# Gated cross-attention: transposes by VectorE and a DRAM round trip in place of TensorE's, and attend in the middle of a step

## The chip, the cores and the metric

One core of a Trainium2 chip. Time is device microseconds of one execution, the median of the runs.

## What is computed

For each of 32 batches, 112 rows of x (512 wide) attend to 375 rows of memory (256 wide), and a gate mixes the result into x. The reference, cut to what matters:

```
memory_proj    = einsum('bme,de->bmd', memory, W_mem)
scores         = einsum('bnd,bmd->bnm', hidden_states, memory_proj) / sqrt(D)
attn           = softmax(scores, axis=-1)
memory_context = einsum('bnm,bmd->bnd', attn, memory_proj)
gate_input     = concatenate([hidden_states, memory_context], axis=-1)
gate           = sigmoid(einsum('bnf,df->bnd', gate_input, W_gate) + b_gate)
fused          = hidden_states + gate * memory_context
out            = rmsnorm(fused, norm_w)        # eps 1e-6
```

All arrays are float32.

## The kernel before

memory_proj is never formed. W_mem is folded into the other side: q = x W_mem, scores = q memory^T, am = softmax(scores) memory (256 wide), context = am W_mem^T, and the gate's attended half is am times wga, a product of the two weights that is made once at the start.

**Precision.** Each float32 operand of a product is split into a high part (ScalarE, `high`) and the remainder (VectorE or GpSimd, `low`, a tensor_tensor that subtracts). Each product is three: high by high, high by low, low by high. A name with `_hi` or `_lo` is such a part, `_raw` what it is made from, and the name without either the thing itself. GpSimd makes memT_lo, mem_lo (one pair a batch) and xT_lo (three units a group); VectorE makes qT_lo, pT_lo and amT_lo.

**Tiling.** Eight batches of 112 rows make a group of 896 columns, which is seven tiles of 128 rows. Scores, softmax and attend go by batch; the gate, context, fuse and norm go by tile. Tile t of a group needs batches up to t+1. There are four groups; the two in the middle are one loop body. q is made in six pieces a group (three units of 256, 320 and 320 columns, two halves each).

**One step of TensorE (batch b)**, in the order in which `group` and `fillers` write it: `score(b)`, `gate_x(b-1)` (the x half of a gate, twelve products), `probs_turn(b)` (three transposes of the probabilities through an identity), `gate_am(b-2)` (the attended half, six products), `attend(b)` (nine products), `context(b-2)` (six), `am_turn(b)` (two transposes). q pieces stand where there is no tile work.

**The other engines in that step.** VectorE: gate_context (work from ctx_ps), amT_low, maximum (top and shift), fuse (work from x_rows), shares (a reciprocal), pT_low, add_bias (work from gate_ps), norm (work from rstd and norm_w), and q_low where there is a piece. ScalarE: the high parts, the exponential with its sum, the scaled copy `am`, tanh and the square with its sum. GpSimd: memT_lo, the inverse root, mem_lo, xT_lo. SP issues all DMAs in one list: a batch's memory (760 KB, both layouts in one transfer), x rows, results, xT.

Each engine runs its own list in order; what ties them are semaphores with constant thresholds (or registers in the loop body). `pT_low` and `amT_low` read the transposes where TensorE left them, in PSUM (`pT_ps`, `am_bank`).

## Time and profile before

| | us |
|---|---|
| median of 3 runs | 296.33 (296.28 to 297.29) |
| span of the profiled execution | 294.5 |
| TensorE busy | 287.4 |
| VectorE busy | 190.2 |
| ScalarE busy | 171.9 |
| GpSimd busy | 161.5 |

The profile is one execution. Its span runs from the first to the last instruction; the timed runs lie 1.8 us above it, which is what surrounds the span. An engine's busy time is the sum of its instructions; neighbouring matrix products overlap, so a group's mean is longer than the pace at which they follow each other. That pace is read from the chain of waits in order of time. The granted clock is the share of TensorE's full speed that the chip allowed in a stretch.

### The profile page before, as it was taken

How to read it: one execution, taken by the hardware profiler on the slowest of the kernel's cores; microseconds unless marked ns; L12 is line 12 of the kernel's file. 1: busy time of each engine (PE TensorE's matmuls, PEld its weight loads, DVE VectorE, ACT ScalarE, POOL GpSimd, SP SyncE). 2: the span in 40 equal slices, each digit the busy share in tenths (PEclk: the TensorE clock that was granted, in tenths of full speed). 3: DMA queues.
4: the chain of work that ended last, by engine and by line, in shares of the span. 5: the costliest groups of instructions: out<-in, count | busy, mean ns of one | idle time of the engine just before them, and what ended most of it. 6: DMA issues, size and time to landing. Idle time of an engine off the chain costs nothing.

```text
span 294.5 us, 4927 instructions
## 1 busy us (share of the span) xinstructions
PE 287.4 (98%) x1639; PEld 251.4 (85%) x1639; DVE 190.2 (65%) x328; ACT 171.9 (58%) x363; POOL 161.5 (55%) x132
## 2 busy tenths in 40 slices
PE   8999999999999999999999999999999999999991
PEld 4989888888899988888899988888889998888881
DVE  3897556787663267687674247777667335787755
ACT  4886757667447555657636555757735656555442
POOL 0002774859828535858945545685981943555312
PEclk9999999999999999999999999999999999999998
DMA  7997357557452634637472550757654233543101
GB/s 277 421 353 233 116 202 267 177 180 241 137 172 71 250 107 123 236 119 255 160 248 71 175 188 25 266 177 235 208 172 147 102 111 106 179 153 97 38 36 71
DMA packets 15571, 50.83 MB, mean 173 GB/s; under 512 B 1729, under 2 KB 1985, under 8 KB 15297
## 3 DMA queue, kind: packets, MB, share of 16 engines
q1 hardware_dynamic: 15552, 50.60, 51.1%
q8 instruction: 10, 0.16, 0.2%
q14 instruction: 9, 0.07, 0.1%
HBM read 43.25 MB, written 7.34 MB: 172 GB/s over the span
## 4 chain that ended last, share of the span: by engine, by line
PE 98%; issue 0%; DVE 0%; DVEq 0%; POOL 0%; POOLq 0%; ACT 0%
PE gate_ps L283 14%; PE gate_ps L285 14%; PE gate_ps L290 13%; PE ctx_ps L290 5%; PE ctx_ps L283 5%; PE ctx_ps L285 5%; PE q_ps L290 4%; PE q_ps L285 4%; PE q_ps L283 4%; PE am_bank L290 4%; PE am_bank L285 4%; PE am_bank L283 4%; PE score_ps L283 4%; PE score_ps L290 4%; PE score_ps L285 4%; PE pT_ps L335 3%
## 5 line engine op out<-in xcount | busy, mean ns | idle before, releaser
L855 POOL TENSOR_TENSOR memT_lo<-mems_raw,memT_hi 128x752 fp32r<-128x752 f32 x30 | 56.2, 1873 | 75.6 <-ACT memT_hi L513 75.6
L855 POOL TENSOR_TENSOR mem_lo<-mems_raw,mem_hi 128x768 fp32r<-128x768 f32 x30 | 56.2, 1873 | 3.5 <-ACT mem_hi L513 3.5
L638 ACT ACTIVATE am<-am_bank,share 112x256 f32<-112x256 f32 x32 | 15.2, 475 | 44.7 <-PE am_bank L290 44.7
L716 DVE SCALAR_TENSOR_TENSOR work<-work,x_rows 128x512 f32<-128x512 f32 (+1 forms) x29 | 40.6, 1404 | 0.6
L670 DVE TENSOR_TENSOR pT_lo<-pT_ps,pT_hi 128x336 fp32r<-128x336 f32 x32 | 16.2, 508 | 35.8 <-ACT pT_hi L513 35.8
L724 DVE SCALAR_TENSOR_TENSOR work<-work,rstd,norm_w 128x512 f32<-128x512 f32 (+1 forms) x29 | 35.2, 1217 | 1.0 <-POOL rstd L916 1.0
L283 PE MATMUL gate_ps<-wgx_hi,xT_hi 128*128 128x512 f32 x112 | 32.5, 399 | 0.0
L285 PE MATMUL gate_ps<-wgx_lo,xT_hi 128*128 128x512 f32 x112 | 31.7, 391 | 0.0
L290 PE MATMUL gate_ps<-wgx_hi,xT_lo 128*128 128x512 f32 x112 | 31.6, 391 | 0.0
L538 ACT ACTIVATE probs<-score_ps,shift 112x375 f32<-112x375 f32 x32 | 18.4, 574 | 22.4 <-DVE shift L684 22.3
L873 POOL TENSOR_TENSOR guarded<-meansq,eps 128x1 f32<-128x1 f32 x27 | 5.1, 189 | 45.9 <-ACT work L545 45.9
L545 ACT ACTIVATE work<-work 128x512 f32<-128x512 f32 (+1 forms) x29 | 17.8, 614 | 21.2 <-DVE work L716 21.2
L855 POOL TENSOR_TENSOR xT_lo<-xT_raw,xT_hi 128x1280 fp32r<-128x1280 f32 (+1 forms) x9 | 29.1, 3230 | 0.0
L709 DVE SCALAR_TENSOR_TENSOR work<-work,ctx_ps 128x512 f32<-128x512 f32 (+1 forms) x28 | 19.0, 677 | 13.9 <-PE ctx_ps L290 12.8
L513 ACT ACTIVATE memT_hi<-mems_raw 128x752 fp32r<-128x752 f32 x32 | 26.4, 826 | 1.0 <-DMA mems_raw<-in_mems 1.0
L513 ACT ACTIVATE mem_hi<-mems_raw 128x768 fp32r<-128x768 f32 x32 | 26.8, 837 | 0.0
L285 PEld LDWEIGHTS gate_ps<-wgx_lo,xT_hi 128*128 128x128 f32 x112 | 21.0, 188 | 4.7
L290 PEld LDWEIGHTS gate_ps<-wgx_hi,xT_lo 128*128 128x128 f32 x112 | 21.0, 188 | 4.6
L703 DVE TENSOR_TENSOR work<-gate_ps,b_gate 128x512 f32<-128x512 f32 (+1 forms) x29 | 19.4, 670 | 7.2 <-PE gate_ps L290 7.1
L670 DVE TENSOR_TENSOR amT_lo<-am_bank,amT_hi 128x224 fp32r<-128x224 f32 x32 | 12.4, 387 | 17.9 <-ACT amT_hi L513 17.9
L682 DVE TENSOR_REDUCE top<-score_ps 112x1 f32<-112x375 f32 x32 | 17.5, 548 | 8.5 <-PE score_ps L290 8.4
L283 PEld LDWEIGHTS gate_ps<-wgx_hi,xT_hi 128*128 128x128 f32 x112 | 19.8, 188 | 1.8
(123 smaller groups left out, 653.1 us busy)
## 6 DMA issues: line engine op xcount, KB each, us to landing
mems_raw<-in_mems SPq DMA_DIRECT2D x32, 760.0 KB, 4.5
x_rows<-in_x SPq DMA_DIRECT2D x28, 256.0 KB, 4.9
out<-work SPq DMA_DIRECT2D x27, 256.0 KB, 5.0
xT_raw<-in_xT SPq DMA_DIRECT2D x7, 640.0 KB, 5.7
xT_raw<-in_xT SPq DMA_DIRECT2D x3, 512.0 KB, 5.1
work<-in_wgT SPq DMA_DIRECT2D x1, 1024.0 KB, 7.2
x_rows<-in_wgT SPq DMA_DIRECT2D x1, 1024.0 KB, 10.3
xT_raw<-in_xT SPq DMA_DIRECT2D x2, 320.0 KB, 5.0
```

What stands on the lines that cost most here:

```text
L283: pe.matmul(out, l_hi, r_hi, start=first and i == 0, stop=False)
L285: pe.matmul(out, l_hi, r_lo, start=False, stop=False)
L290: mm = pe.matmul(out, l_lo, r_hi, start=False, stop=last and i == len(lefts) - 1)
L513: return act.activation(out, in_, ACT.Copy)
L538: act.activation(probs[:, b % 2, 0:KEYS], scores[:, 0:KEYS], ACT.Exp, bias=shift[:, b % 2:b % 2 + 1], scale=D ** -0.5, accum_out=total[:, ...
L545: act.activation(squares[:, cols], h[:, t % 2, cols], ACT.Square, scale=D ** -0.5, accum_out=meansq[:, slot:slot + 1]).then_inc(meansq_rea ...
L670: return dve.tensor_tensor(out, in_, high.bitcast(F32), ALU.subtract)
L703: dve.tensor_tensor(z[:, t % 2, cols], gate_ps[t % 2][:, cols], b_gate[:, cols], ALU.add).then_inc(z_ready, 1)
L709: dve.scalar_tensor_tensor(out=u[:, cols], in0=z[:, t % 2, cols], scalar=1.0, in1=bank[:, cols], op0=ALU.add, op1=ALU.mult).then_inc(u_rea ...
L716: dve.scalar_tensor_tensor(out=h[:, t % 2, cols], in0=u[:, cols], scalar=0.5, in1=x_rows[:, t % X_SLOTS, cols], op0=ALU.mult, op1=ALU.add) ...
L724: dve.scalar_tensor_tensor(out=y[:, t % 2, cols], in0=h[:, t % 2, cols], scalar=rstd[:, t % 2:t % 2 + 1], in1=norm_w[:, cols], op0=ALU.mul ...
L855: return pool.tensor_tensor(out, in_, high.bitcast(F32), ALU.subtract)
```

## The change

Both transposes leave TensorE. VectorE transposes within blocks of 32 x 32 (`turn_p`, `turn_am`) and writes them in an order that makes the rest a matter of whole rows; SP writes that to a scratch tensor in DRAM and reads it back with the blocks at their places (`write_p`, `read_p`, `write_am`, `read_am`). The result lands in partitions in the order (row in block, block), so the host lays memory and W_mem out in the same order (`turned_rows`). ScalarE and VectorE then split `pT_raw` and `amT_raw` from SBUF, 384 columns in place of 336 and 256 in place of 224.

```diff
-            def probs_turn(g, b):
-                pe.wait_ge(probs_ready, GROUP * g + b + 1)
-                for c in range(KC):
-                    mm = pe.transpose(probsT[:, c], probs[:, b % 2, c * P:(c + 1) * P], ident[0:ROWS, 0:ROWS])
-                mm.then_inc(pT_done, 1)
...
-            def am_turn(g, b):
-                pe.wait_ge(am_ready, GROUP * g + b + 1)
-                for c in range(EC):
-                    mm = pe.transpose(amT_ps[:, c], am[:, c * P:(c + 1) * P], ident[0:ROWS, 0:ROWS])
-                mm.then_inc(amT_done, 1)
...
+            def turn_p(n):
+                dve.wait_ge(probs_ready, n + 1)
+                if n > 0:
+                    dve.wait_ge(p_written, 16 * n)
+                dve.transpose(turned_p, probs_blocks).then_inc(blocks_p_ready, 1)
...
+            def turn_am(n):
+                dve.wait_ge(am_ready, n + 1)
+                if n > 0:
+                    dve.wait_ge(am_written, 16 * n)
+                dve.transpose(turned_am, am_blocks).then_inc(blocks_am_ready, 1)
...
+            def write_p(n):
+                sp.wait_ge(blocks_p_ready, n + 1)
+                sp.dma_start(turned_p_d[n % 2], blocks_p[:]).then_inc(p_written, 16)
+
+            def read_p(n):
+                sp.wait_ge(p_written, 16 * (n + 1))
+                if n >= 1:
+                    sp.wait_ge(pT_lo_ready, n)
+                sp.dma_start(pT_flat, turned_p_d[n % 2].rearrange("(q i) (j n) -> (i j) q n", q=Q, j=Q)).then_inc(p_read, 16)
...
-            dve.wait_ge(pT_hi_ready, GROUP * g + b + 1)
-            low(pT_lo[:, b % 2], probsT, pT_hi[:, b % 2]).then_inc(pT_lo_ready, 1)
+                dve.wait_ge(pT_hi_ready, n + 1)
+                low(pT_slot(pT_lo, n), pT_rows, pT_slot(pT_hi, n)).then_inc(pT_lo_ready, 1)
```

The groups are no longer loops. Steps are numbered through from 0 to 34, batch s has its scores in step s, and its attend in step s + 1. The tile finished in step s is t = `tile_at(s)`: none where s mod 8 is 3. PSUM has a third gate bank in place of `pT_ps`, so that gate_x can run two tiles ahead. TensorE's steps, then VectorE's and SP's:

```diff
+            for s in range(OPENING, STEPS):
+                t = tile_at(s)
+                if s < BATCHES:
+                    score(s)
+                if t is not None and t + 2 < ALL_TILES:
+                    gate_x(t + 2)
+                if s <= BATCHES:
+                    attend(s - 1)
+                for g, unit, half in q_pieces_at(s):
+                    q_piece(g, unit, half)
+                if t is not None:
+                    gate_am(t)
+                    if t < LAST:
+                        context(t)
...
+            for s in range(OPENING, STEPS):
+                if tile_at(s - 2) is not None:
+                    finish(tile_at(s - 2))
+                if s - 2 < BATCHES:
+                    write_am(s - 2)
+                    read_am(s - 2)
+                if s < BATCHES:
+                    write_p(s)
+                if s + 2 < BATCHES:
+                    load_memT(s + 2)
+                if s + 1 < BATCHES:
+                    load_mem(s + 1)
+                if s < BATCHES:
+                    read_p(s)
+                if x_load_at(s) is not None and s != 2:
+                    load_xT(*x_load_at(s))
```

q pieces stand at s mod 8 = 0, 1, 3 (two), 6 and 7. GpSimd splits a unit of xT at s mod 8 = 1, 4 and 7. In the opening the memory loads come earlier, `load_memT(2)` ahead of wgx and of xT's third unit, and the first scores stand between the products of the weights. At the end, attend(31) stands in step 32 and gate_am of the last tile in step 34.

TensorE, one step in the middle of a group with a tile and no q piece, before (L283, L285 and L290 are the high-high, high-low and low-high products of every kind):

```order
L283 MATMUL score_ps<-memT_hi,qT_hi 112x376 x2
L285 MATMUL score_ps<-memT_lo,qT_hi 112x376 x2
L290 MATMUL score_ps<-memT_hi,qT_lo 112x376 x2
L283 MATMUL gate_ps<-wgx_hi,xT_hi 128x512 x4
L285 MATMUL gate_ps<-wgx_lo,xT_hi 128x512 x4
L290 MATMUL gate_ps<-wgx_hi,xT_lo 128x512 x4
L335 MATMUL pT_ps<-ident,probs 128x112 x3
L283 MATMUL gate_ps<-wga_hi,amT_hi 128x512 x2
L285 MATMUL gate_ps<-wga_lo,amT_hi 128x512 x2
L290 MATMUL gate_ps<-wga_hi,amT_lo 128x512 x2
L283 MATMUL am_bank<-mem_hi,pT_hi 112x256 x3
L285 MATMUL am_bank<-mem_lo,pT_hi 112x256 x3
```

and now, from score on:

```order
L353 MATMUL score_ps<-memT_hi,qT_hi 112x376 x2
L355 MATMUL score_ps<-memT_lo,qT_hi 112x376 x2
L360 MATMUL score_ps<-memT_hi,qT_lo 112x376 x2
L353 MATMUL gate_ps<-wgx_hi,xT_hi 128x512 x4
L355 MATMUL gate_ps<-wgx_lo,xT_hi 128x512 x4
L360 MATMUL gate_ps<-wgx_hi,xT_lo 128x512 x4
L353 MATMUL am_bank<-mem_hi,pT_hi 112x256 x3
L355 MATMUL am_bank<-mem_lo,pT_hi 112x256 x3
L360 MATMUL am_bank<-mem_hi,pT_lo 112x256 x3
L353 MATMUL q_ps<-xT_hi,wm_hi 128x256 x4
L355 MATMUL q_ps<-xT_lo,wm_hi 128x256 x4
L360 MATMUL q_ps<-xT_hi,wm_lo 128x256 x4
```

The transposes are gone, and attend stands ahead of the gate's attended half (here with a q piece between them).

VectorE, from gate_context of one tile to the pT_lo behind it, before:

```order
L709 SCALAR_TENSOR_TENSOR work<-work,ctx_ps 128x512
L670 TENSOR_TENSOR amT_lo<-am_bank,amT_hi 128x2x112
L681 REGISTER_ALU
L682 TENSOR_REDUCE top<-score_ps 112x1
L684 TENSOR_SCALAR shift<-top 112x1
L716 SCALAR_TENSOR_TENSOR work<-work,x_rows 128x512
L689 RECIPROCAL share<-total 112x1
L670 TENSOR_TENSOR pT_lo<-pT_ps,pT_hi 128x336
```

and now:

```order
L737 SCALAR_TENSOR_TENSOR work<-work,ctx_ps 128x512
L722 STREAM_TRANSPOSE blocks_am<-am 128x2x4x32
L688 TENSOR_TENSOR amT_lo<-amT_raw,amT_hi 128x2x128
L700 TENSOR_REDUCE top<-score_ps 112x1
L702 TENSOR_SCALAR shift<-top 112x1
L744 SCALAR_TENSOR_TENSOR work<-work,x_rows 128x512
L708 STREAM_TRANSPOSE blocks_p<-probs 128x3x4x32
L712 RECIPROCAL share<-total 112x1
L688 TENSOR_TENSOR pT_lo<-pT_raw,pT_hi 128x384
```

Two block transposes stand in that stretch that were not there, and amT_lo and pT_lo read SBUF where they read PSUM; pT_lo is that of the batch before.

SP, one step with a load of xT in it, before:

```order
L200 DMA mems_raw<-in_mems 128x1520
L196 DMA xT_raw<-in_xT 128x1280
L210 DMA x_rows<-in_x 128x512
L250 DMA out<-work 128x512
L200 DMA mems_raw<-in_mems 128x1520
```

and a step now:

```order
L268 DMA x_rows<-in_x 128x512
L275 DMA out<-work 128x512
L259 DMA turned_am<-blocks_am 128x256
L265 DMA amT_raw<-turned_am 128x4x64
L249 DMA turned_p<-blocks_p 128x384
L240 DMA memT_raw<-in_memT 128x752
L245 DMA mem_raw<-in_mem 128x768
L255 DMA pT_raw<-turned_p 128x4x96
```

Each read-back waits on SP for its write to land, and the next write stands behind it.

## Rows read from the trace of the kernel before

**Rows 1.** The page: TensorE's busy time, share and instructions; its granted clock by slice
```profile
PE 287.4 (98%) x1639; PEld 251.4 (85%) x1639; DVE 190.2 (65%) x328; ACT 171.9 (58%) x363; POOL 161.5 (55%) x132
PEclk9999999999999999999999999999999999999998
```
**Rows 2.** The page: the chain that ended last, share of the span by engine
```profile
PE 98%; issue 0%; DVE 0%; DVEq 0%; POOL 0%; POOLq 0%; ACT 0%
```
**Rows 3.** The same chain in order of time: start us, us on the path, engine and tile
```profile
61.67 0.35 PE score_ps L283 x2
...
62.72 0.92 PE gate_ps L283 x4
...
65.45 0.29 PE pT_ps L335 x3
...
67.14 0.35 PE am_bank L283 x3
...
68.20 0.45 PE ctx_ps L283 x2
...
69.56 0.19 PE am_bank L354 x2
...
77.86 0.49 PE q_ps L283 x4
...
83.49 0.59 PE q_ps L283 x4
...
147.10 0.49 PE q_ps L283 x4
```
**Rows 4.** The timeline of one step: start us, us, engine, line, operation, [idle before]
```profile
200.08 0.68 DVE L709 SCALAR_TENSOR_TENSOR work<-work,ctx_ps 128x512 f32<-128x512 f32 x1
...
201.24 0.55 DVE L682 TENSOR_REDUCE top<-score_ps 112x1 f32<-112x375 f32 x1 [0.18 <-PE score_ps L290]
...
201.35 1.81 POOL L855 TENSOR_TENSOR memT_lo<-mems_raw,memT_hi 128x752 fp32r<-128x752 f32 x1 [1.75 <-ACT memT_hi L513]
...
201.82 0.15 DVE L684 TENSOR_SCALAR shift<-top 112x1 f32<-112x1 f32 x1
...
202.00 1.71 DVE L716 SCALAR_TENSOR_TENSOR work<-work,x_rows 128x512 f32<-128x512 f32 x1
...
202.01 0.58 ACT L538 ACTIVATE probs<-score_ps,shift 112x375 f32<-112x375 f32 x1 [0.74 <-DVE shift L684]
...
205.66 0.69 DVE L703 TENSOR_TENSOR work<-gate_ps,b_gate 128x512 f32<-128x512 f32 x1 [0.32 <-PE gate_ps L290]
...
206.27 1.45 DVE L724 SCALAR_TENSOR_TENSOR work<-work,rstd,norm_w 128x512 f32<-128x512 f32 x1
```
**Rows 5.** VectorE's timeline between two groups, where GpSimd has nothing to subtract
```profile
152.03 0.74 DVE L724 SCALAR_TENSOR_TENSOR work<-work,rstd,norm_w 128x512 f32<-128x512 f32 x1
...
153.75 0.68 DVE L716 SCALAR_TENSOR_TENSOR work<-work,x_rows 128x512 f32<-128x512 f32 x1
```
**Rows 6.** VectorE's groups by form: xcount | busy us, mean ns | idle before
```profile
L670 DVE TENSOR_TENSOR pT_lo<-pT_ps,pT_hi 128x336 fp32r<-128x336 f32 x32 | 16.2, 508 | 35.8 <-ACT pT_hi L513 35.8
...
L670 DVE TENSOR_TENSOR mem_lo<-mems_raw,mem_hi 128x768 fp32r<-128x768 f32 x2 | 1.9, 948 | 0.0
...
L734 DVE CAST xT_hi<-first_raw 128x512 fp32r<-128x512 f32 x1 | 0.4, 428 | 3.3 <-DMA first_raw<-in_first 3.3
```
**Rows 7.** DMA queues (packets, MB, busy share) and issues (KB each, us to landing)
```profile
q1 hardware_dynamic: 15552, 50.60, 51.1%
...
out<-work SPq DMA_DIRECT2D x27, 256.0 KB, 5.0
...
out<-work SPq DMA_DIRECT2D x2, 128.0 KB, 1.7
```
**Rows 8.** The timeline: the first split of wgx, and the last gate's products
```profile
14.53 1.14 ACT L513 ACTIVATE wgx_hi<-x_rows 128x512 fp32r<-128x512 f32 x2
...
286.54 0.62 PE L290 MATMUL gate_ps<-wga_hi,amT_lo 128*128 128x512 f32 x2
```

845 lines of the change are left out of this document (425 added, 420 removed).

## The prediction

> **What bounds the kernel now.** I read the busy shares first. TensorE is busy for 98% of the span, VectorE for 65%, ScalarE for 58%, GpSimd for 55%, and TensorE's granted clock stands at its upper level throughout [rows 1]. Then the chain of waits that ends last: TensorE has 98% of it, waiting and issuing nothing [rows 2]. So the kernel is TensorE's instruction list laid end to end, and what leaves that list shortens it, provided that nothing else becomes late. One step (a batch with a tile, without a q piece) takes 8.1 us (score at 61.67, the next behind the transposes at 69.56 + 0.19) and a group of eight batches 69.24 us (77.86 to 147.10), in the chain's order of time [rows 3]. Last I read VectorE's timeline: how long its chain from one gate to the next probabilities is, and what stretches it [rows 4, 5].
>
> **What is removed.** Per batch three transposes of probs (0.29 us) and two of am (0.19 us) on the path: 0.48 us, by 32 batches 15.4 us [rows 3]. TensorE's own work is then 7.62 us in a plain step (score 3 x 0.35, gate_x 3 x 0.92, attend 3 x 0.35, gate_am and context 3 x 0.46 each, less rounding), 65.4 in a group (69.24 - 8 x 0.48). The Trainium skill ("VectorE: DVE Perf Modes", section The three transpose paths) gives a TensorE transpose of 128x128 as 390 ns and VectorE's 32x32-block form as 311 ns, and its rules say to transpose 128x128 on TensorE where PSUM will do. The trace has them at 0.29 / 3 = 0.10 us each on the path, so by the page's figure 62 us would be won, by the row a quarter of it. The row decides.
>
> **What is added on VectorE.** Per batch a block transpose of 384 columns and one of 256. No row shows one. From below the CAST of 512 columns at 428 ns bounds it (384 columns: about 0.33 us). From above two passes over the data: the 768-column subtraction from SBUF at 948 ns (256 columns: 0.68). I take one pass, as VectorE's tensor_tensor rows go, 508 ns for 336 columns and 690 for 512, so 1.04 ns a column: 0.56 and 0.42 us [rows 4, 6]. pT_lo grows from 336 columns to 384 (0.56) and amT_lo from 224 to 256 (0.42), and both now read two SBUF tensors, where they read PSUM and SBUF.
>
> That last point has a price that the rows show. fuse and norm read two SBUF tensors. With GpSimd idle they take 0.68 and 0.74 us [rows 5]. With a GpSimd subtraction under way, fuse started at 202.00 ended at 203.71, that is 0.55 us behind the end (201.35 + 1.81) of memT_lo, and norm took 1.45 [rows 4]. add_bias and gate_context, which read PSUM, stay at 0.69 beside the same GpSimd work. So a two-SBUF operation waits until GpSimd's instruction ends. The block transposes have one input and should not.
>
> **What the new order does.** Before, gate_am(b-2) and a half of the gate stand between the probabilities and attend. Now attend(s-1) stands behind score(s) and gate_x(t+2), and VectorE issues pT_low(s-1) behind maximum(s), fuse, turn_p(s) and shares(s). So a loop closes every step: attend, gate_am, context, then VectorE's gate_context down to pT_low, then attend again. I lay it out from zero = end of gate_am(t-1), with the durations above; instructions back to back start 0.08 before the end of the last (205.66 + 0.69 = 206.35, next at 206.27) [rows 4].
> - TensorE: context ends 1.38, score(s) 2.42, gate_x 5.19, the six attend products that need no pT_lo 5.89.
> - VectorE: add_bias 0.04 to 0.73; norm to 1.40; gate_context waits for context, 1.42 to 2.11; turn_am to 2.46; amT_low to 2.80; maximum and shift to 3.45.
> - ScalarE: tanh to 1.4, am 1.8, amT_hi 2.1, memT_hi 2.85; exp 3.46 to 4.14 with its accumulator read.
> - GpSimd starts memT_lo(s+1) at 2.85 and holds until 4.67. fuse, ready at 3.48, ends 4.67 + 0.55 = 5.22. turn_p 5.14 to 5.71, the reciprocal hidden but for 0.08, pT_low(s-1) 5.71 to 6.27.
> - TensorE's last three attend products thus start at 6.3 in place of 5.89, and with gate_am's 1.38 the next zero is at 8.2.
>
> So the plain step takes 8.2 us, where TensorE alone wants 7.62 and before took 8.10: the saving is gone. A q piece lies inside the loop and adds its own 1.77 (3 x 0.59) or 1.45 us (3 x 0.49) [rows 3] to both sums, 10.0 and 9.65.
>
> Two places in a group are worse. **The step without a tile** (s mod 8 = 3) has neither gate_x nor gate_am. VectorE's pT_low(2) still comes at 6.27, while TensorE is through at 3.1; then two q pieces, their q_low and norm on VectorE, and score, gate_x, attend and gate_am of the next step. From gate_am(2) to gate_am(4) I get 17.2 us against 13.3 of TensorE's own. **The splits of xT** on GpSimd (3.4 us each, behind mem_lo) at s mod 8 = 1 and 7 reach 2.2 to 2.4 us past the next zero. norm waits for them, gate_context stands behind norm, amT_low then meets memT_lo: 1.3 and 1.4 us more. The one at 4 has no norm behind it and costs nothing.
>
> A group: 8.2 (s = 5) + 9.5 (2) + 11.4 (0) + 10.0 (1) + 2 x 9.65 (6, 7) + 17.2 (3 and 4) = 75.6 us, against 69.24.
>
> **The round trips.** turn_p(s) ends at 5.71; ScalarE wants its copy behind exp(s+1), at 8.2 + 4.15, so 6.6 us are there. A store of 128 KB with the queue empty lands 1.7 us after issue, one of 256 KB behind other loads 5.0 [rows 7]. So write plus read take 3.4 to 10 us. I take 5.5: the write 2.2, the read 3.3, as 760 KB of memory are issued ahead of it and the 50.6 MB so far keep the queues 51% busy (at that pace 760 KB take 2.3 us). That is hidden with 1.1 us to spare. SP's list is in order too: behind write_am(s-2) and its landing stands write_p(s). read_am is issued at about 5.1, before write_p is due. The second trip (am) has a whole step and is hidden, except at the end.
>
> **Opening.** load_memT(2) waits for VectorE's split of memT(0) (about 11 us) and stands ahead of the loads of wgx and xT unit 2, so wgx, split from 14.53 on before [rows 8], arrives at about 16. TensorE's list up to gate_am(0) sums to 40.3 us; I add 5.7 for gate_x(0) (0.8), attend(0) and q piece 2 (1.9) and score(3), whose memory split stands behind read_p(1) on ScalarE (3). So 46.
>
> **Tail.** After attend(31) nothing covers the trip of am: am, block transpose, write, read, two copies take until 8.4 us past gate_am(25) and the last three gate products 0.6 more. Before, the last gate ended at 286.54 + 0.62 = 287.2 [rows 8], 7.3 before the end of the span, and that part is unchanged.
>
> **The sum.** 46 + 27.5 (s = 5, 6, 7) + 3 x 75.6 - 2.9 (no q pieces in the last group) + 6.6 (s = 32) + 9.0 + 7.3 = 320.3 us of span. The medians lie 1.8 above the profiled span (296.3 against 294.5): **322 us**.
>
> **Rivals.**
> 1. *TensorE stays the bound, as intended: faster.* If turn_p(s) or pT_low is never late, each group costs 65.4. With opening and tail as above that is 290, with a clean opening 284: take **288**. It decides when pT_low(s-1) ends before 5.9 in the step. For it: TensorE never waited before, and VectorE idled 35.8 us before pT_lo alone [rows 6]. Against it: that idle time was 1.1 us a step, and the change puts 0.56 + 0.42 us of transposes into just that stretch.
> 2. *The waits for GpSimd fall elsewhere: about even.* If fuse meets no GpSimd work, pT_low ends at 5.3 and plain steps run at 7.62, but the step without a tile still loses 2.2. The group is 67.8, the total **297**, hence no change. It decides when memT_lo(s+1) begins after fuse.
> 3. *The round trip becomes the bound.* At 10 us, two trips of the loop take 10 + 0.55 + 0.56 + 0.54 + 1.38 + 5.71 = 18.7, or 9.4 a step, 1.2 over mine, by 28 steps +33: **355**. For it: 21 MB more through the queues, half of it in pieces of 384 and 256 bytes, and five more issues a step on SP. Against it: the 1.7 us row.
> 4. *Block transposes at their other bounds.* 0.33 and 0.3 us make it 314, 0.95 and 0.68 make it 340.
>
> **Chances.** My forecast, rival 4 inside it (305 to 335): 0.47. Rival 3, 335 and above: 0.20. Rival 2 (293 to 305): 0.13. Rival 1 (282 to 293): 0.20. The range of 286 to 345 leaves out a third of rival 1 and half of rival 3. A measurement of this kernel can tell about 0.5%, 1.5 us. Faster by more: 0.20 plus a fifth of rival 2, 0.23. Within: 0.07. Slower: 0.70.
>
> **What would show it.** Right: TensorE busy under 92%; waits of am_bank products for VectorE's pT_lo of about 0.4 us in plain steps and 3 us once in eight; pT_lo and amT_lo with means over their 0.56 and 0.42; VectorE over 80% busy. Rival 1: TensorE at 98% again. Rival 3: ScalarE's pT_hi waiting for the DMA of pT_raw. A granted clock below its upper level in mid-kernel would add to any of them and is in none of my numbers.

## The result and the profile of the changed kernel

The changed kernel takes 358.5 us (median of 6 runs, 354.4 to 360.5) against 296.3 before: 1.205 times as long, 95% interval 1.200 to 1.211. The direction of the prediction (slower) was right; its time, 322 us, was not, and its range ended at 345. The profiled execution took 354.4 us with a span of 352.3, so the sum to compare with is the predicted span, 320.3: 32.0 us are unexplained. Ratios and intervals here and below are over the fast runs, those within 1.5% of a kernel's fastest, and for an experiment without its profiled run, so they need not equal the quotient of two medians, and one experiment has too few such runs for any.

The page of the changed kernel, busy times and granted clock in 40 slices, then the chain that ended last by engine and its largest DMA shares (before: [rows 1, 2]):

```profile
PE 294.3 (84%) x1479; PEld 248.5 (71%) x1479; DVE 213.3 (61%) x388; ACT 172.9 (49%) x363; POOL 163.7 (46%) x135
...
PE   8939759999799769889799769888979779989973
...
PEclk9996998999899899999999989999989988999998
...
DMA packets 63191, 71.87 MB, mean 204 GB/s; under 512 B 37056, under 2 KB 45504, under 8 KB 62912
...
PE 29%; DMA 23%; DVE 21%; issue 16%; ACT 7%; SPq 2%; DVEq 0%; POOL 0%; POOLq 0%; ACTq 0%
```

TensorE fell from 98% busy to 84% though it has 160 instructions fewer, and from 98% of the chain to 29%. No engine took its place: VectorE is busy 61%. The path now goes round through all of them, with DMA in it for 23%. TensorE's busy time even rose, from 287.4 to 294.3 us, without the 15 us of transposes: its clock was granted at the lower level for part of the time (mean 0.953 against 0.995).

The waits: engine, line, tile, what was waited for; us in total, times, longest. First the engines', then SyncE's own:

```profile
PE am_bank L353 <- ACT pT_hi L532: 33.5, 19, 4.7
...
ACT memT_hi L532 <- DMA memT_raw<-in_memT: 12.1, 9, 2.1
...
ACT amT_hi L532 <- DMA amT_raw<-turned_am: 8.1, 3, 5.3
...
ACT pT_hi L532 <- DMA pT_raw<-turned_p: 7.5, 7, 1.9
PE am_bank L360 <- DVE pT_lo L688: 7.0, 13, 0.9
...
PE gate_ps L353 <- DVE wgx_lo L688: 5.5, 1, 5.5
```

```profile
SPq L265 <- DMA turned_am<-blocks_am: 84.5, 31, 6.5
SPq L275 <- DVE work L752: 51.6, 21, 5.4
SPq L255 <- DMA turned_p<-blocks_p: 27.6, 31, 6.3
```

TensorE waits at attend's first product, and mostly for ScalarE's pT_hi, not for VectorE's pT_lo as I had it. SyncE spends 112 us of the span waiting for a write to land before it may issue the read of the same rows (L265, L255).

Where the 32.0 us are, by the starts of add_bias on VectorE's timeline (each is the end of a gate_am):

| stretch | predicted | measured |
|---|---|---|
| to gate_am(0), step 4 | 46 | 57.7 |
| steps 5, 6, 7 | 8.2 + 9.65 + 9.65 = 27.5 | 8.4 + 9.8 + 9.8 = 27.9 |
| steps 8 to 31 | 3 x 75.6 - 2.9 = 223.9 | 82.7 + 81.9 + 78.8 = 243.4 |
| step 32, last gates, tail | 6.6 + 9.0 + 7.3 = 22.9 | 7.3 + 8.7 + 7.3 = 23.3 |

So the misses are the opening (11.7 us) and 6.5 us in each group.

### The profile page after: what moved, and what is told of

Its sections match the earlier page's. It is cut to its first block, busy times and chain, and to the rows that moved or that the text cites. A ratio compares the mean times of both kernels' runs of the same rounds, so it can differ in the third digit from the quotient of the medians.

```text
span 352.3 us, 4693 instructions
## 1 busy us (share of the span) xinstructions
PE 294.3 (84%) x1479; PEld 248.5 (71%) x1479; DVE 213.3 (61%) x388; ACT 172.9 (49%) x363; POOL 163.7 (46%) x135
## 2 busy tenths in 40 slices
DMA packets 63191, 71.87 MB, mean 204 GB/s; under 512 B 37056, under 2 KB 45504, under 8 KB 62912
## 4 chain that ended last, share of the span: by engine, by line
PE 29%; DMA 23%; DVE 21%; issue 16%; ACT 7%; SPq 2%; DVEq 0%; POOL 0%; POOLq 0%; ACTq 0%
DMA turned_am<-blocks_am 9%; DMA turned_p<-blocks_p 7%; DMA pT_raw<-turned_p 5%; PE am_bank L360 4%; PE gate_ps L353 3%; DVE work L731 3%; PE q_ps L355 3%; PE q_ps L353 3%; PE gate_ps L360 3%; PE gate_ps L355 3%; PE q_ps L360 3%; ACT work L588 3%; DVE top L700 3%; DVE blocks_am L722 3%; DVE blocks_p L708 3%
## 5 line engine op out<-in xcount | busy, mean ns | idle before, releaser
L872 POOL TENSOR_TENSOR memT_lo<-memT_raw,memT_hi 128x752 fp32r<-128x752 f32 x31 | 58.1, 1873 | 100.7 <-ACT memT_hi L532 100.7
L872 POOL TENSOR_TENSOR mem_lo<-mem_raw,mem_hi 128x768 fp32r<-128x768 f32 x32 | 59.7, 1864 | 16.6 <-ACT mem_hi L532 16.6
L353 PE MATMUL am_bank<-mem_hi,pT_hi 128*112 128x256 f32 x96 | 18.9, 307 | 33.5 <-ACT pT_hi L532 33.5
L353 PEld LDWEIGHTS am_bank<-mem_hi,pT_hi 128*112 128x112 f32 x96 | 14.1, 182 | 42.4 <-ACT pT_hi L532 41.2
L688 DVE TENSOR_TENSOR qT_lo<-q_ps,qT_hi 128x320 fp32r<-128x320 f32 (+1 forms) x22 | 10.4, 472 | 51.6 <-ACT qT_hi L532 51.5
L532 ACT ACTIVATE memT_hi<-memT_raw 128x752 fp32r<-128x752 f32 x32 | 26.4, 826 | 12.1 <-DMA memT_raw<-in_memT 12.1
L532 ACT ACTIVATE qT_hi<-q_ps 128x320 fp32r<-128x320 f32 (+1 forms) x22 | 9.3, 421 | 37.3 <-PE q_ps L360 36.7
L532 ACT ACTIVATE mem_hi<-mem_raw 128x768 fp32r<-128x768 f32 x32 | 26.6, 830 | 0.0
L360 PE MATMUL am_bank<-mem_hi,pT_lo 128*112 128x256 f32 x96 | 19.9, 320 | 7.1 <-DVE pT_lo L688 7.0
L708 DVE STREAM_TRANSPOSE blocks_p<-probs 128x384 f32<-128x384 f32 x32 | 18.3, 572 | 12.0 <-ACT probs L561 7.6
```

What stands on the lines that cost most here:

```text
L353: pe.matmul(out, l_hi, r_hi, start=first and i == 0, stop=False)
L360: mm = pe.matmul(out, l_lo, r_hi, start=False, stop=last and i == len(lefts) - 1)
L532: return act.activation(out, in_, ACT.Copy)
L708: dve.transpose(turned_p, probs_blocks).then_inc(blocks_p_ready, 1)
L872: return pool.tensor_tensor(out, in_, high.bitcast(F32), ALU.subtract)
```

## The experiments

The whole table first; "group" is the mean of the three times from the first gate of a group to the first of the next, and "first gate" the start of the first add_bias, both from VectorE's timeline of the one profiled run. With the trips in, the three differ (72.5, 79.2 and 79.3 us in the run G, 75.4, 81.6 and 73.3 in G, O); without them they agree to 0.2 us, but for T, O (73.0, 74.6 and 74.5). O: pT's split first on ScalarE and VectorE. G: GpSimd's work cut short. T: no round trips.

| run | us (range of runs) | ratio to before, interval | first gate | group |
|---|---|---|---|---|
| before | 296.3 | | 34.9 | 69.2 |
| changed | 358.5 (354.4 to 360.5) | 1.205, 1.200 to 1.211 | 57.7 | 82.2 |
| O | 342.3 (337.1 to 346.2) | 1.159, 1.152 to 1.166 | 54.6 | 77.9 |
| G | 339.9 (336.3 to 343.6) | none | 56.6 | 77.0 |
| T | 341.7 (339.7 to 342.8) | 1.152, 1.147 to 1.157 | 47.5 | 82.0 |
| G, O | 339.8 (339.2 to 340.8) | 1.145, 1.142 to 1.147 | 58.5 | 76.8 |
| T, O | 317.4 (316.9 to 318.9) | 1.071, 1.067 to 1.075 | 48.5 | 74.0 |
| T, G | 300.2 (298.9 to 301.7) | 1.014, 1.009 to 1.018 | 47.5 | 68.4 |
| T, G, O | 293.7 (293.0 to 294.3) | 0.990, 0.988 to 0.993 | 47.9 | 66.4 |

### No round trips (T)

```
             def turn_p(n):
                 dve.wait_ge(probs_ready, n + 1)
-                if n > 0:
-                    dve.wait_ge(p_written, 16 * n)
-                dve.transpose(turned_p, probs_blocks).then_inc(blocks_p_ready, 1)
+                if n > 1:
+                    dve.wait_ge(pT_lo_ready, n - 1)
+                dve.transpose(turned_p[n % 2], probs_blocks).then_inc(blocks_p_ready, 1)
...
             def pT_high(n):
-                act.wait_ge(p_read, 16 * (n + 1))
-                high(pT_slot(pT_hi, n), pT_rows).then_inc(pT_hi_ready, 1)
+                act.wait_ge(blocks_p_ready, n + 1)
+                high(pT_slot(pT_hi, n), pT_rows[n % 2]).then_inc(pT_hi_ready, 1)
```

> Left out: both round trips through DRAM. ScalarE and VectorE read VectorE's block transposes of the probabilities and of the attended rows where they lie in SBUF (two buffers each), so the 32x32 blocks stay unshuffled; every operation of every engine is otherwise the changed kernel's, in its order, and SyncE's list loses its four round-trip transfers a step. Three readings of the 358.5 us. (A) The time beyond the 322 us of the prediction comes from the round trips and from SyncE's list, in which a write waits behind the bulk loads and they behind it: about 36 us go and some 318 to 328 us are left, attend's wait for pT_hi (33.5 us, 19 times in the profile) falling below 10. (B) It comes from the order on ScalarE and VectorE: pT_high(s-1) stands behind exp(s), so attend waits with or without DRAM: 345 us or more. (C) The VectorE loop too was only bound through the transfers: under 308 us.

Measured 341.7 us, between reading A (318 to 328) and B (345 or more). The edit takes several things out together: the transfers, their 21 MB, SyncE's waits and the block transposes' waits for a write. Of the 13.2 us between the two profiled spans (352.3 and 339.1) 10.2 lie in the opening, where the first gate comes at 47.5 us, near my 46, instead of 57.7, and 2.3 behind the third group. The groups did not get shorter, 82.0 us against 82.2. So in the loop of the changed kernel the round trips cost nothing as long as everything else is as it is, and something else makes the group 6.4 us longer than my 75.6. Its steps repeat to a tenth, so they can be read against mine: 8.3, 9.8, 9.8 as predicted (8.2, 9.65, 9.65), but 13.5 at s mod 8 = 0 (predicted 11.4), 11.8 at 2 (9.5) and 18.7 over 3 and 4 (17.2).

The timeline of step 8 of this run: start us, us, engine, line, operation, [idle before, released by]:

```profile
75.53 2.96 POOL L854 TENSOR_TENSOR xT_lo<-xT_raw,xT_hi 128x1280 fp32r<-128x1280 f32 x1 [1.26 <-ACT xT_hi L512]
...
75.96 3.08 DVE L734 SCALAR_TENSOR_TENSOR work<-work,rstd,norm_w 128x512 f32<-128x512 f32 x1
...
78.46 2.25 POOL L854 TENSOR_TENSOR memT_lo<-memT_raw,memT_hi 128x752 fp32r<-128x752 f32 x1
78.97 0.67 DVE L719 SCALAR_TENSOR_TENSOR work<-work,ctx_ps 128x512 f32<-128x512 f32 x1
...
79.93 1.07 DVE L670 TENSOR_TENSOR amT_lo<-amT_raw,amT_hi 128x256 fp32r<-128x256 f32 x1
80.92 0.53 DVE L682 TENSOR_REDUCE top<-score_ps 112x1 f32<-112x375 f32 x1
...
81.68 0.57 ACT L541 ACTIVATE probs<-score_ps,shift 112x375 f32<-112x375 f32 x1 [3.57 <-DVE shift L684]
...
82.24 0.51 ACT L512 ACTIVATE pT_hi<-pT_raw 128x384 fp32r<-128x384 f32 x1
...
82.80 0.98 PE L333 MATMUL am_bank<-mem_hi,pT_hi 128*112 128x256 f32 x3 [2.38 <-ACT pT_hi L512]
...
83.59 0.84 PE L335 MATMUL am_bank<-mem_lo,pT_hi 128*112 128x256 f32 x3
84.23 0.84 PE L340 MATMUL am_bank<-mem_hi,pT_lo 128*112 128x256 f32 x3
```

norm stands on VectorE until GpSimd is through with xT_lo, amT_lo runs into memT_lo, and maximum reads scores that were ready over 3 us earlier. exp(s) is late, and pT_high(s-1), whose input has been there for a step, stands behind exp(s) on ScalarE: TensorE waits 2.38 us. VectorE's part of this chain was in my working, with pT_lo as its last link; pT_hi as the last was not. Nor was the end: three attend products take 0.84 us here and 0.51 in an undisturbed step. TensorE alone in 2 us stretches: PE busy, granted clock, DMA share:

```profile
80.00:82.00 2.00, 0.42 (x2) 1.00 1.03 342
82.00:84.00 2.00, 1.20 (x5) 0.68 0.79 216
84.00:86.00 2.00, 2.00 (x11) 0.50 0.21 81
86.00:88.00 2.00, 2.00 (x13) 0.97 0.00 0
```

Behind the wait the clock was granted at its lower level (0.50, that is 1.2 of 2.4 GHz) until about 86 us.

### GpSimd's work cut short (G)

```
-                    split_memT(s + 1)
+                    n = s + 1
+                    pool.wait_ge(memT_hi_ready, n + 1)
+                    low(memT_lo[:, n % 2, :, 0:16], memT_raws[:, n % 2, :, 0:16], memT_hi[:, n % 2, :, 0:16]).then_inc(memT_lo_ready, 1)
```

(and likewise mem_lo and xT_lo, in the loop from step 4)

> Left out: from step 4 on GpSimd subtracts 16 columns of each chunk of memT, mem and xT instead of all, so nearly all of its 163.7 us of busy time in the changed kernel goes; the parts not subtracted keep older values. All else is the changed kernel. By the prediction's step that VectorE's operations on two SBUF operands wait for GpSimd: fuse and norm fall from 1.34 and 1.27 us to about 0.7 (28 of each: 35 us of VectorE's time, of which at least the 0.24 a step above the 0.45 free of the loop is on the path: 6 us), norm's 3.1 us in xT steps goes (8 times 1.8 us on the path), and score no longer waits for memT_lo: some 20 to 30 us less, 330 to 340. If the path runs through the round trips and GpSimd's waits lie beside it, under 8 us go: 350 us or more.

339.9 us: 18.6 less, at the upper end of the first theory (330 to 340); its four runs lie in two pairs, 336.3 and 337.2, 342.6 and 343.6, so the gain is known to a few us only. VectorE's groups, us busy and mean ns: fuse and norm of the changed kernel, and of this run:

```profile
L744 DVE SCALAR_TENSOR_TENSOR work<-work,x_rows 128x512 f32<-128x512 f32 x27 | 36.2, 1342 | 0.0
L752 DVE SCALAR_TENSOR_TENSOR work<-work,rstd,norm_w 128x512 f32<-128x512 f32 x27 | 34.2, 1266 | 0.4 <-POOL rstd L892 0.4
```

```profile
L752 DVE SCALAR_TENSOR_TENSOR work<-work,rstd,norm_w 128x512 f32<-128x512 f32 x27 | 20.1, 743 | 0.4 <-POOL rstd L892 0.4
L744 DVE SCALAR_TENSOR_TENSOR work<-work,x_rows 128x512 f32<-128x512 f32 x27 | 18.6, 691 | 0.0
```

Both fall to what [rows 5] show beside an idle GpSimd, while the block transposes, with one input, do not move (572 and 437 ns before, 578 and 439 here). The Trainium skill states that rule ("SBUF — State Buffer", section Who interferes with whom): a VectorE instruction with two SBUF inputs contends with a GpSimd instruction that reads SBUF, one with at most one SBUF input, outside the two-port modes, does not. The two pairs of rows agree. The plain steps fell to 7.6 us, TensorE's own time, but others stayed at 11 to 13 us, now with ScalarE waiting 1.84 us for memT_raw and 1.13 us for pT_raw in one step. GpSimd out of the way, the transfers showed. TensorE waits for GpSimd's own results only once in either kernel, 2.1 us for the same memT_lo in the opening, so what the edit took away in the loop had reached TensorE by way of VectorE, or of buffers that came free late for the next load.

### Both (T, G)

> Left out: both round trips through DRAM (the engines read the block transposes as they lie, blocks unshuffled) and, from step 4, all but 16 columns of each chunk of GpSimd's subtractions. Order and all else are the changed kernel's. Each alone took 17 to 19 us off 358.5. If the two losses stand in different places they add: 358.5 - 16.8 - 18.6 = 323 us. If each hides the other (in the run without GpSimd's work the step of s mod 8 = 0 was long again, 13.1 us, now through memT_raw and pT_raw that came late) more goes than the sum: 305 to 315 us. If a third cause, the order of ScalarE's and VectorE's lists, holds the loop by itself: 330 us or more.

300.2 us: 58 us below the changed kernel, where the two alone gave 17 and 19, and below even the 305 to 315 that I expected if each hid the other's cost. So each does. With both out, the group is 68.4 us; take the trips back in and it is 77.0, take GpSimd back in and it is 82.0, take both and it is 82.2. VectorE's lateness and the trips' lateness lie side by side in the same wait of attend.

### The order of ScalarE's and VectorE's lists (O)

```
+                if s - 1 < BATCHES:
+                    pT_low(s - 1)
                 if before is not None:
                     fuse(before)
                 if s < BATCHES:
                     turn_p(s)
                     shares(s)
-                if s - 1 < BATCHES:
-                    pT_low(s - 1)
```

(and pT_high(s-1) ahead of split_memT(s+1) and exponentials(s) on ScalarE)

> Order alone: ScalarE's pT_high(s-1) goes ahead of its split of memT(s+1) and exp(s), VectorE's pT_lo(s-1) ahead of fuse and of the block transpose of step s; nothing left out. If attend waits because pT_high stands behind a late exp(s) (ScalarE's and VectorE's order): its waits for pT_hi and pT_lo (33.5 and 7.0 us) shrink by half and 12 to 25 us go, 333 to 346 us. If attend waits because the round trip itself lands late (ScalarE waited 7.5 us for pT_raw where pT_high stood behind exp(s)), pT_high now holds exp(s) back and the time stays within 8 us of 358, on either side.

> As the run before it (no round trip, GpSimd's subtractions cut from step 4), and in addition pT_high(s-1) ahead of memT's split and exp(s) on ScalarE, and pT_lo(s-1) ahead of fuse and of the block transpose on VectorE. If the order of these two lists is what holds the loop once transfers and GpSimd are out of the way, the plain step falls from 8.3 to TensorE's own 7.6 us and 10 to 20 us more go, to 295 to 310 us. If the order matters only because pT is late for another reason, it gains under 4 us here.

> Left out: both round trips (block transposes are read as they lie, unshuffled); GpSimd does all its work; pT_high(s-1) and pT_lo(s-1) stand first. So far: the changed kernel 358.5, order alone 342.3, no round trip alone 341.7, short GpSimd alone 339.9, the last two together 300.2, all three 293.7. With the round trips gone what is left of the loss is GpSimd's and the lists': if pT's early split takes attend off the VectorE list that waits for GpSimd, the three steps of a group with an xT split or a late norm shrink and the time is 300 to 312 us, beside the 308.0 of TensorE's turns with the same order. If GpSimd's hold on VectorE reaches attend in another way (memT_lo and mem_lo late, maximum late): 325 us or more.

> Left out: GpSimd's subtractions but for 16 columns of each chunk from step 4; the round trips stay; pT_high(s-1) and pT_lo(s-1) stand first. With GpSimd out of the way what is left of the loss is the round trip's lateness behind SyncE's list. The order can't hasten a transfer: if that is the whole rest, the time stays at 330 to 340 us, near the 339.9 of the run without the order. If VectorE, free sooner, hands its block transposes over sooner so that the transfers land in time: 305 to 320 us.

Alone the order gives 16.2 us; without trips 24.3 (341.7 to 317.4), without trips and GpSimd 6.5, and with the trips but no GpSimd nothing that the spread of G's runs would let one see (339.9 to 339.8). Two of the four expectations missed: without trips and GpSimd I had 10 to 20 us, and without trips 300 to 312 us in all. In the run T, O TensorE still waits 18.7 us for pT_lo, up to 3.0 at a time. That is the pattern of a list that waits for GpSimd: with pT_lo first, GpSimd's hold falls on norm (mean 1687 ns, fuse 685 in the run O), where attend feels it less. And where the transfer is what is late, ScalarE only stands before it instead of TensorE: in the run G, O its wait for pT_raw is 66.7 us. T, G, O is the change as it was meant: plain steps of 7.6 us, TensorE 95% busy, group 66.4 us. Even that is only 1% faster than before (0.990, 0.988 to 0.993), since its first gate comes at 47.9 us instead of 34.9.

### Turns by TensorE again, attend still in mid-step

```
             def turn_p(n):
+                pe.wait_ge(probs_ready, n + 1)
+                if n > 0:
+                    pe.wait_ge(pT_lo_ready, n)
+                for c in range(KC):
+                    mm = pe.transpose(pT_rows[:, c], probs[0:ROWS, n % 2, c * P:(c + 1) * P], ident[0:ROWS, 0:ROWS])
+                mm.then_inc(pT_done, 1)
...
                     attend(s - 1)
+                if s - 2 < BATCHES:
+                    turn_am(s - 2)
+                if s < BATCHES:
+                    turn_p(s)
```

> One part of the change undone: TensorE turns the probabilities and the attended rows (five transposes a step into PSUM) and nothing goes through DRAM; attend(s-1) stays in mid-step behind the gate's x product, and the flat step loop stays. PSUM holds no third gate bank, so the gate's x product runs one tile ahead instead of two; ScalarE and VectorE evacuate attended rows one step earlier than in the changed kernel since both share a bank. If the turns are the whole cost and the place of attend is harmless: 290 to 305 us, TensorE busy 93% or more. If the place of attend costs by itself (pT_high(s-1) behind exp(s) on ScalarE, pT_lo late): 315 us or more.

In this first form the attended rows were turned ahead of score(s). 344.7 us (1.162, 1.160 to 1.164); TensorE waited 27.9 us at that turn, so it tested its own place for the turn more than the change, though it fell where the second theory had it (315 or more). The second form, as in the diff:

> TensorE turns the probabilities and attended rows as in the run of 344.7 us, but the attended rows are turned behind attend(s-1), one step later, so that ScalarE and VectorE evacuate them with the changed kernel's lag. In that run TensorE waited 0.5 to 0.9 us in nearly every step (27.9 us, 30 times) at the first weight load of the attended rows' turn, which stood ahead of score(s): if those waits were its 8.8 us plain step, 20 to 25 us go (320 to 325 us) and the place of attend costs the remaining 25 over the kernel before. If the place of attend costs nothing itself: 300 us or less. If those waits hid others: 335 us or more.

> As the run before it (turns by TensorE with the changed kernel's lag, no DRAM), and pT_high(s-1) ahead of memT's split and exp(s) on ScalarE, pT_lo(s-1) ahead of fuse on VectorE: so pT(s-1), which stands in PSUM since the step before, is split during the score and no longer behind exp(s). If the mid-step attend is slow only through these two lists, TensorE is busy over 95% in mid-kernel and the time is 296 to 308 us, within a few us of the kernel before plus its longer opening (first add_bias at 51 instead of 35 us costs what it costs). If the mid-step place itself costs (GpSimd's late memT_lo and mem_lo, norm and fuse): 315 us or more.

The second form took 326.4 us (1.102, 1.098 to 1.105): with no block transposes and no trips, the place of attend, the lists and the opening cost 30 us. The first gate has 10.4 us of it (45.3 against 34.9), the three groups 21.9, and the end is 4.0 shorter. Its steps are 8.3, 9.7, 9.7, 11.4, 10.0, 9.7, 17.3 in the second and third group, 76.0 us, near my layout of 75.6 almost step for step. That is in part luck: a step of this kernel has five transposes more on TensorE and two operations fewer on VectorE than the one that I laid out. Its clock stays up but for one fall, in the first group, which takes 77.6 us. With pT first, 308.0 us (1.039, 1.037 to 1.040), at the end of the 296 to 308 of the first theory: plain steps of 8.1 and a group of 70.8 against 69.2 before. What then remains over the kernel before is the first gate at 45.5 us instead of 34.9, and 4.9 us in the three groups, less 4.3 at the end. So attend in mid-step costs little once its input does not stand behind exp(s) and fuse.

### The clock

```
                 if s <= BATCHES:
+                    if s % GROUP in (0, 2, 3) and s > GROUP - 1:
+                        pe.wait_ge(am_ready, s - 1)
+                        for i in range(FILL):
+                            pe.matmul(am_bank[:], wm_hi[:, i % DC, 0:P], wgx_hi[:, i % DC], start=True, stop=True)
                     attend(s - 1)
```

> No round trips (blocks unshuffled) and the changed kernel's order, as in the run of 341.7 us; added: from step 8 on, in steps s mod 8 = 0, 2 and 3, eight TensorE products of 128x512 between two constant weight tiles into the attended rows' bank, ahead of attend's wait for pT_hi; attend overwrites them. In that run TensorE waited 2.2 to 2.4 us in each of these steps, and behind the wait the granted clock was 0.50 for 2 to 3 us (attend's matmuls 0.84 us per three instead of 0.51). The eight products take some 2.2 us and stand in the wait. If the lower clock comes from the wait itself and is what the prediction left out of these steps (13.5, 11.8, 18.7 us measured, 11.4, 9.5, 17.2 predicted): the granted clock stays 1.0 there, the three steps lose about 1.2 us each (3.5 to 5 us a group) and the time falls by 10 to 15 us to 326 to 332. If the clock is not what made them long, the products only add their own time: 342 to 350 us.

329.7 us (1.112, 1.109 to 1.114), 12.0 less than without the products, as the first theory said. The same step, the products and then attend, and the clock:

```profile
80.09 1.98 PE L502 MATMUL am_bank<-wgx_hi,wm_hi 128*128 128x512 f32 x8
82.66 0.39 PEld L334 LDWEIGHTS am_bank<-mem_hi,pT_hi 128*112 128x112 f32 x3 [1.02 <-ACT pT_hi L517]
...
83.10 0.51 PE L336 MATMUL am_bank<-mem_lo,pT_hi 128*112 128x256 f32 x3
```

```profile
82.00:84.00 2.00, 1.40 (x12) 1.00 0.89 278
84.00:86.00 2.00, 2.00 (x14) 1.00 0.11 42
```

With the wait filled the clock stayed at 1.00 and three attend products took 0.51 us. The three long steps became 12.0, 10.3 and 17.3 us, nearer my 11.4, 9.5 and 17.2: most of what my layout lacked in them was the clock. The Trainium skill's row on this ("TensorE: Matmul & The Clock Gate", section Why this matters for your kernels) warns of throughput drops after TensorE has idled between bursts in mid-kernel. The stretches of the two runs agree with that in kind (0.50 behind the wait of 2.38 us, 1.00 where it was filled).

A wait of such a length does not always bring the lower clock. In the run T, G TensorE waits 2.24 or 2.25 us for pT_hi once in each group, and behind all three waits the clock is 1.00. The first of them, then the clock in the stretch behind it:

```profile
104.03 0.61 PE L333 MATMUL am_bank<-mem_hi,pT_hi 128*112 128x256 f32 x3 [2.24 <-ACT pT_hi L512]
...
104.00:106.00 2.00, 1.97 (x15) 1.00 0.82 283
```

In the second form with TensorE's turns it waits 1.87 us at the same place in each group; behind the first the clock fell to 0.50 for over 2 us, behind the other two it stayed at 1.00. What decides between the two, no run here shows.

> The changed kernel with nothing left out, and eight TensorE products of 128x512 between constant weight tiles ahead of attend's wait in steps s mod 8 = 0, 2 and 3 from step 8 on (attend overwrites them). If the clock is a cost of its own beside the trips, the time falls as without trips, by 8 to 14 us, to 344 to 350 us. If the trips' late landings decide when attend's inputs are there whatever TensorE's clock, so that the faster matmuls only wait longer: within 4 us of 358.5.

With the trips in, the same products bring 353.7 us (1.194, 1.190 to 1.198), 4.8 us less, between the two theories. In the profiles the nine steps with products are 7.9 us shorter together than in the changed kernel, and the six steps with s mod 8 = 5, 6 and 7 behind them 5.2 us longer. What the clock gives back there is in good part waited away afterwards.

### What makes the trips late

> Nothing left out; the change with three edits of order: pT_high(s-1) and pT_lo(s-1) first; from step 4 on the bulk loads of memT, mem and xT issued by ScalarE behind its split of mem, so that SyncE's list holds only round trips, x and out; in the opening wgx_low(2) and wgx_low(3) ahead of the second block transpose, which waited 3.0 us for the first write to land behind the queued loads. Order alone gave 342.3 us. If SyncE's list delayed the round trips (5.2 us in each xT step), 10 to 20 us more go, and the opening gives 2 to 4: 318 to 330 us. If the round trips are late because of the transfers in front of them in the rings and not of the list, only the opening's part goes: 338 us or more. Slower than the kernel before either way.

357.7 us (1.202, 1.195 to 1.209): 15 us worse than the order alone. Moving the bulk loads to ScalarE's queue did not let the trips pass. In its profile the write of turned_p lands 4.8 us after issue (median), 2.1 with one queue, and SyncE waits 126.7 us for it instead of 27.5. Its read lands sooner, 2.6 us in place of 3.9, so by the medians a trip takes 7.4 us instead of 6.0; for the attended rows the two landings are 3.0 and 3.6 us in place of 2.9 and 2.1. My guess is that the write now shares the DMA engines with two loads that were behind it before. No run shows this alone: that run changed three things at once, so the next ones change less, on top of O or of G, O.

The timeline of SyncE, VectorE and ScalarE around a late step of the run G, O:

```profile
153.42 0.50 SPq L234 DMA_DIRECT2D xT_raw<-in_xT  x1
...
155.86 0.33 SPq L259 DMA_DIRECT2D turned_am<-blocks_am  x1
...
159.57 0.58 DVE L708 STREAM_TRANSPOSE blocks_p<-probs 128x384 f32<-128x384 f32 x1
...
163.50 0.37 SPq L265 DMA_DIRECT2D amT_raw<-turned_am  x1
...
163.91 0.50 SPq L249 DMA_DIRECT2D turned_p<-blocks_p  x1
...
166.28 0.38 SPq L255 DMA_DIRECT2D pT_raw<-turned_p  x1
...
171.25 0.52 ACT L532 ACTIVATE pT_hi<-pT_raw 128x384 fp32r<-128x384 f32 x1 [5.12 <-DMA pT_raw<-turned_p]
```

The write of the attended rows is issued behind a 640 KB load of xT and lands 7 us later. Until then SyncE stands at read_am, and write_p, due at 160.15, is issued at 163.91; its read then needs 5 us more, and attend stands.

```
                 if s - 2 < BATCHES:
                     write_am(s - 2)
+                if s < BATCHES:
+                    write_p(s)
+                if s - 2 < BATCHES:
                     read_am(s - 2)
-                if s < BATCHES:
-                    write_p(s)
+                if s < BATCHES:
+                    read_p(s)
                 if s + 2 < BATCHES:
                     load_memT(s + 2)
                 if s + 1 < BATCHES:
                     load_mem(s + 1)
-                if s < BATCHES:
-                    read_p(s)
```

> Nothing left out. pT_high and pT_lo first (342.3 us so far), and from step 4 on SyncE's list in another order: write_am, write_p, read_am, read_p, and only then the loads of memT and mem; so no read's wait for its own write holds the other write back, and no bulk load of the same step is in the rings ahead of a trip. If SyncE's list is what makes pT_raw late, ScalarE's wait for it (62.6 us, 26 times) falls under 25 us and the time to 318 to 330 us. If the transfers are late through the load on the DMA engines itself, 338 us or more; the loads, issued later, can also become late themselves: 345 us or more.

> Left out: GpSimd's subtractions but for 16 columns of each chunk from step 4. Order as in the run with pT first and short GpSimd (339.8 us), with SyncE's list changed as in the run before this. With GpSimd out of the way, what stands between 339.8 and 293.7 (no trips either) is the trips' lateness, of which some 10 us lie in the opening that this edit leaves alone. If the list is the cause in the loop: 303 to 315 us. If it is the load on the DMA engines: 330 us or more.

333.9 us on O (1.126, 1.119 to 1.132; 8.4 less) and 329.6 on G, O (1.110, 1.105 to 1.115; 10.2 less). ScalarE's wait for pT_raw falls from 62.6 to 25.1 us, but its waits for amT_raw rise from 8.7 to 36.0 and for memT_raw, now issued last, to 23.6. The list is worth 8 to 10 us, where I had expected 12 to 24 and 25 to 37 if it were the whole cause; the rest stays.

```
-                sp.dma_start(pT_flat, turned_p_d[n % 2].rearrange("(q i) (j n) -> (i j) q n", q=Q, j=Q)).then_inc(p_read, 16)
+                sp.dma_start(pT_raw[:], turned_p_d[n % 2]).then_inc(p_read, 16)
```

(and likewise the read of the attended rows)

> Left out: GpSimd's subtractions but for 16 columns of each chunk from step 4; and the shuffle, since both reads take the rows from DRAM as they were written (the same bytes, runs of 1536 and 1024 bytes instead of 384 and 256), so that the blocks stay unshuffled. Otherwise the run of 339.8 us. If the reads' small packets load the DMA engines and so delay every transfer, their time falls, the DMA share with it, and 10 to 25 us go: 315 to 330 us. If only bytes, the list and the two landings of each trip count: 335 us or more.

331.1 us (1.120, 1.113 to 1.128), 8.7 less than G, O; packets fell from 63191 to 38615 with the same 71.87 MB. The small packets thus cost about as much as the list, less than the 10 to 25 us of the first theory. The Trainium skill ("DMA: Bandwidth & Descriptors", section Specifications) asks for transfers of at least 512 bytes for full rate. The pair agrees in kind, though the median landing of pT_raw hardly moved (4.2 to 4.0 us).

> Nothing left out. pT_high and pT_lo first (342.3 us so far); in the opening wgx_low(2) and wgx_low(3) go ahead of the second block transpose of probabilities; and these transposes alternate between two buffers, so that one waits for the write before the last instead of the last. In the profile of the changed kernel the second transpose waited 3.0 us and the third 0.9 us for a write, and TensorE stood 5.45 us before the first gate product and ran it at half clock. If that wait is the opening's excess, the first bias add moves from 54.6 us to 48 to 51 us and the time to 335 to 339 us. If the reads' landings (pT_raw, amT_raw) set it whatever the transposes do, it moves by under 2 us.

347.2 us (1.162, 1.152 to 1.172), no gain on the order's 342.3. TensorE's wait before the first gate product shrank from 5.45 us in the changed kernel to 2.02, and the first gate still came at 56.2 us: TensorE then waited 4.56 us for pT_hi at 51.77, where it had waited 4.71 at 53.57. So the block transpose that waits for a write is not what bounds the opening. Without any trips the first gate came at 47.5 to 48.5 us; whether SyncE's list or the landings of trips 0 to 3 make the difference, no run separates.

> Nothing left out: pT_high and pT_lo first, SyncE's list with both writes ahead of the reads and the loads of memT and mem behind them, and the eight products in steps s mod 8 = 0, 2 and 3. The first two gave 333.9 us. With pT first the steps of s mod 8 = 0 and 2 took 10.0 to 10.8 and 7.7 to 9.4 us there, so the waits that the products should fill are mostly gone: 2.2 us of products in such a step would add up to 1.5 us. If the clock still counts: 322 to 330 us. If the products only add their time: 335 to 342 us. Slower than the kernel before in each case.

335.5 us (1.132, 1.128 to 1.137), not to be told from the 333.9 without the products, so the second theory holds. No version of the change that computes everything came nearer to the kernel before than 1.126; with TensorE's turns it was 1.039.

## Why the prediction was wrong, step by step

The profiled span missed my 320.3 us by 32.0. Taking the trips out removes 13.2 of them (352.3 to 339.1), filling three waits a group 11.4 more (339.1 to 327.7), and 7.4 remain, of which 6.0 are 2.0 a group (77.6 against 75.6). So two steps failed, the round trips and the clock, the first for the opening, the second for the loop. The shares go with this order of taking out: with the trips in, the products gave only 4.8 us.

**What bounds, what is removed: right.** With trips, GpSimd's work and the late split of pT all taken out, the plain step is 7.6 us and the group 66.4, against my 7.62 and 65.4 of TensorE's own. What rival 1 (288 us) describes then takes 293.7.

**Block transposes: right.** 572 and 437 ns against 0.56 and 0.42 us. pT_lo, at 569 ns, hardly lies over its 0.56; amT_lo, at 489, does over its 0.42.

**The loop through VectorE and its waits for GpSimd: right in mechanism and size.** Plain steps 8.3 against 8.2 in the run T (8.4, 9.1 and 9.2 in the changed kernel), and 7.6 in the runs G and T, G; steps 5 to 7 at 27.9 against 27.5. The layout without the clock, 75.6 a group, was measured at 77.6 with the trips out and the waits filled. I named one wrong engine in it: TensorE waited for ScalarE's pT_hi, mostly behind exp(s), for 33.5 us and for VectorE's pT_lo for 7.0 (0.9 us at most, where I had 3 us once in eight), and VectorE is 61% busy, not over 80%.

**The clock: a term put at nothing, and the second step that failed.** I wrote that a clock below its upper level was in none of my numbers. My own layout had TensorE idle for 2 to 3 us in three steps of a group, and no reason why the clock should stay up there. Filled, these waits gave 4.4 us a group and 12.0 in all without trips, 4.8 with them. This is most of the 6.4 us a group in which the run without trips lies over my sum.

**The round trips, "hidden with 1.1 us to spare": the first step that failed.** I sized one trip at 5.5 us from the landings of single transfers and the 760 KB ahead of it, where 6.6 were free. The medians were 2.3 and 4.0 us, 6.3 together, still inside, but the median is not what counts: writes behind large loads land 5 to 7 us after issue, and SyncE's list hands that on to the other trip. The 640 KB load of xT was in none of my sums. I had looked at the list in the plain step alone ("read_am is issued at about 5.1, before write_p is due"). The cost fell in the **opening**, 10.2 us (57.7 against 47.5 without trips, my 46), where over 3 MB of loads had been issued in the 6 us before the first write and it needed 7.1 us to land. There TensorE waited 5.45 us instead of 2.56 before its first gate products and 4.71 us, instead of not at all, before attend(3), and its clock stood at 0.50 behind both waits (in the run T behind the first only). In the loop the trips came to nothing beside GpSimd's waits (82.2 and 82.0), and to about 9 us a group as soon as these were gone (77.0 against 68.4). A cost called hidden was hidden behind another that I counted too; only the runs with both taken out show either at its size.

**Rival 3**, the trips as the bound at 355 us, has nearly the measured number and half the mechanism. Without trips 341.7 us remain. **Rival 2** (297) was not about even: fuse met no GpSimd work in the runs O (685 ns) and G (691 ns), and they took 342.3 and 339.9 us. Only with the trips out as well did it come near, 300.2. The opening's 46 held to 2.5 us where trips were out of the opening, and the tail's 7.3 held.

The rest of the 358.5: the changed kernel's runs spread over 6 us and the profiled one was the shortest, 4.1 below the median, so these 4.1 us are in no profile. Not tried: a write and a read of the two trips on a queue of their own, and another order of the trips in the opening. How the cost of the trips in the loop divides between the bytes and the two landings stays open.

## What to carry to other kernels

When a change puts two new lateness sources on one wait, price each with the other taken away; "hidden" means hidden behind something that may itself be a loss. Read an in-order DMA list at its worst step (the largest load ahead of a small write that someone reads back) and not at the median landing. And where a layout leaves TensorE idle for about as long as here (1.9 to 2.4 us), give the slower clock of the work behind it a price and a chance: it came behind some of these waits and not behind others.

## What the runs showed of the hardware that I had not expected

- With the bulk loads on a second issuing queue, 192 KB writes landed after 4.8 us instead of 2.1, their reads after 2.6 instead of 3.9. Two other edits were in the same run, so the cause is not shown.
- TensorE's clock fell to 0.50 behind waits of 2.38 us (run T) and once of 1.87 us, and stayed at 1.00 behind three waits of 2.24 and 2.25 us (run T, G).
- Kernels with the round trips differ by 0.5 to 3.6% from run to run (337.1 to 346.2 us for O, 327.7 to 339.5 with SyncE's order); those without them by less than 1% (293.0 to 294.3 us for T, G, O).
- Doing useless work paid: eight products in each of three waits a group took 12.0 us off a kernel of 341.7, by the clock alone (mean 0.944 without them, 0.991 with them).
